# One transformer layer on one core: the norms applied by ScalarE, and a longer running sum on VectorE in one attention chunk

## The reference

```python
paths = sigmoid(x @ Wp + bp)                       # 8 heads x 5 levels
agree = pq * pk + (1 - pq) * (1 - pk)
sim   = cumprod(agree, -1).sum(-1) / 5             # causal mask, then
ctx   = softmax(sim) @ (x @ Wv)
x = layernorm(x + ctx @ Wo)
h = silu(x @ wg.T) * (x @ wu.T)                    # 768 wide
x = layernorm(x + h @ wd.T)
# layernorm(x) = (x - mean) / sqrt(var + 1e-5), over the 256 columns
```

## Time and profile before

| what | value |
|---|---|
| median of 3 runs | 849.27 us (848.09 to 849.35) |
| the profiled execution's own time | 848.94 us |
| its span | 847.1 us |
| PE busy | 802.3 us (95%) |
| DVE busy | 613.9 us (72%) |
| ACT busy | 456.4 us (54%) |
| POOL busy | 293.4 us (35%) |

### The profile page before, as it was taken

How to read it: one execution, slowest core, us unless ns; L and a number is a source line. 1 busy time by engine, 2 the same in 40 slices (tenths; PEclk the granted TensorE clock), 3 DMA queues, 4 the chain that set the end, 5 groups by cost and what they waited for, 6 DMA issues and landing times.

```text
span 847.1 us, 14414 instructions
## 1 busy us (share of the span) xinstructions
PE 802.3 (95%) x5538; PEld 397.6 (47%) x5538; DVE 613.9 (72%) x1101; ACT 456.4 (54%) x721; POOL 293.4 (35%) x266
## 2 busy tenths in 40 slices
PE   6998999999999999999999999999999998999886
PEld 5553364444634455453644536444454444444253
DVE  2767966778667876679666795677766787667966
ACT  1656736556465654657455573655646464465422
POOL 0201522436225262244413462142622425234424
PEclk9999999999999999999999999999999999999998
DMA  7932462042610636006630247105260063400001
GB/s 226 208 105 75 100 160 91 1 103 77 171 50 1 150 83 166 1 6 146 147 102 1 60 91 186 64 1 117 84 150 1 1 150 91 109 1 2 26 0 52
DMA packets 47510, 71.02 MB, mean 84 GB/s; under 512 B 3920, under 2 KB 26704, under 8 KB 47440
## 3 DMA queue, kind: packets, MB, share of 16 engines
q1 hardware_dynamic: 47440, 70.07, 31.7%
HBM read 53.28 MB, written 16.78 MB: 83 GB/s over the span
## 4 chain that ended last, share of the span: by engine, by line
PE 57%; DVE 25%; issue 9%; ACT 5%; POOL 1%; DMA 1%; SPq 0%; DVEq 0%; POOLq 0%; ACTq 0%
PE slot L879 10%; PE misc L960 9%; PE ctx_ps L902 9%; PE misc L853 7%; PE misc L948 7%; PE misc L925 6%; DVE acc L600 5%; PE den_ps L908 5%; DVE work L700 5%; ACT probs L504 4%; DVE x L683 3%; DVE acc L597 3%; DVE x1T_lo L690 2%; PE misc L862 2%; DVE ctx_raw L610 1%
## 5 line engine op out<-in xcount | busy, mean ns | idle before, releaser
L504 ACT ACTIVATE probs<-slot 128x1024 f32<-128x1024 f32 (+3 forms) x384 | 290.2, 808 | 290.4 <-PE slot L879 261.9
L433 POOL TENSOR_SCALAR_AFFINE_SELECT probs<-probs 128x512 f32<-128x512 f32 x128 | 145.9, 1140 | 207.7 <-ACT probs L504 207.5
L447 POOL TENSOR_TENSOR work<-work 128x512 f16<-128x512 f32 x96 | 116.1, 1209 | 177.4 <-ACT work L522 177.4
L902 PE MATMUL ctx_ps<-probs,vz_sb 128*32 128x512 f32 (+3 forms) x1536 | 164.5, 501 | 4.8 <-DVE ctx_raw L610 2.6
L879 PE MATMUL slot<-query_stack,key_stack 128*128 128x512 f16 (+3 forms) x768 | 160.6, 330 | 1.6 <-ACT probs L504 1.0
L948 PE MATMUL misc<-x1T_hi,w_parts 128*128 128x512 f16 x358 | 136.1, 380 | 8.5 <-DVE x1T_lo L690 6.0
L948 PE MATMUL misc<-x1T_lo,w_parts 128*128 128x512 f16 x358 | 135.8, 379 | 0.0
L879 PEld LDWEIGHTS slot<-query_stack,key_stack 128*128 128x128 f16 x768 | 56.6, 98 | 161.6 <-issue 126.2
L600 DVE TENSOR_TENSOR acc<-acc,probs 128x1536 f32<-128x1536 f32 (+3 forms) x64 | 106.5, 1664 | 1.3 <-POOL probs L433 1.1
L700 DVE SCALAR_TENSOR_TENSOR work<-work,misc 128x512 f32<-128x512 f32 x90 | 61.4, 682 | 59.7 <-ACT work L516 59.7
L960 PE MATMUL misc<-w_parts,work 128*128 128x256 bf16 x720 | 84.8, 274 | 2.4 <-POOL work L447 2.0
(11 more groups left out here) (81 smaller groups left out, 738.4 us busy)
## 6 DMA issues: line engine op xcount, KB each, us to landing
key_stack<-phi_dram SPq DMA_DIRECT2D x56, 256.0 KB, 5.8
query_stack<-phi_dram SPq DMA_DIRECT2D x56, 256.0 KB, 6.6
x_sb<-in_x_dram SPq DMA_DIRECT2D x8, 1024.0 KB, 5.3
out_dram<-x SPq DMA_DIRECT2D x15, 512.0 KB, 4.5
xT_sb<-in_xT_dram SPq DMA_DIRECT2D x7, 1024.0 KB, 4.9
phi_dram<-phi_hi SPq DMA_DIRECT2D x14, 256.0 KB, 2.0
phi_dram<-phi_lo SPq DMA_DIRECT2D x14, 256.0 KB, 2.3
key_stack<-phi_dram SPq DMA_DIRECT2D x16, 128.0 KB, 3.1
```

Of the source, the lines that this page charges most:

```text
L433: pool.affine_select(out=tile, in_=tile, compare_op=ALU.is_ge, fill=0.0, base=0, pattern=[[0, 4], [1, P]], channel_multiplier=-1).then_inc ...
L447: pool.tensor_tensor(hid_lo[:, n % M1, :], hid[:, n % HSLOTS, :], hid_hi[:, n % M1, :], ALU.subtract).then_inc(hid_lo_ready, 1)
L504: act.activation(probs[:, s % P_SLOTS, 2 * p:2 * p + 2, off:CH], slot[p][:, :, off:CH], ACT.Exp).then_inc(slot_drained[p], 1)
L902: mm = pe.matmul(ctx_ps[32 * k:32 * k + 32, off:CH], vz_sb[:, b % 2, j, 32 * h:32 * h + 32], probs[:, s % P_SLOTS, k, off:CH], start=first ...
```

## The change

`apply` moves from DVE to ACT: four ACT instructions on 128x256 rows compute `rstd * x + shift`, with the two factors read from per-partition tiles. DVE makes the shift, `-mean * rstd`, in one small instruction at the place in its queue where `apply` stood. The two-row `apply_half` of the very end stays on DVE. Apart from that, `ADD_FROM` for pass 2 goes from 3 to 1.

```diff
-    ADD_FROM = {2: 3, 3: 1}
+    ADD_FROM = {2: 1, 3: 1}
...
+            def apply(ln, b, c):                       # ScalarE
+                act.wait_ge(shift_ready, NORM[ln, b, c] + 1)
+                for t in range(TC):
+                    row = x1[:, TC * c + t, :]
+                    act.activation(row, row, ACT.Identity, bias=mean_scaled[:, t:t + 1],
+                                   scale=rstd[:, t:t + 1]).then_inc(ln_done, 1)
...
-            def apply(ln, b, c):                       # VectorE
+            def shift(ln, b, c):
                 dve.wait_ge(rstd_ready, NORM[ln, b, c] + 1)
-                for t in range(TC):
-                    row = x1[:, TC * c + t, :]
-                    dve.tensor_scalar(row, row, mv[:, t, 0:1], rstd[:, t:t + 1],
-                                      ALU.subtract, ALU.mult).then_inc(ln_done, 1)
+                dve.scalar_tensor_tensor(out=mean_scaled[:, :], in0=mv[:, :, 0], scalar=-1.0, in1=rstd[:, :],
+                                         op0=ALU.mult, op1=ALU.mult).then_inc(shift_ready, 1)
```

More of the change, by code:

```diff
@@ L253, in seq_postln_kernel @@
         rstd = sb("rstd", [P, TC], F32)
+        mean_scaled = sb("mean_scaled", [P, TC], F32)
         w_max = sb("w_max", [P, 4], F32)
@@ L308, in seq_postln_kernel @@
         rstd_ready = sem("rstd_ready")
+        shift_ready = sem("shift_ready")
         ln_done = sem("ln_done")
@@ L538, in _ @@
                     hidden_hi(*n)
+                elif what == "apply":
+                    apply(*n)
         @block.vector
@@ L800, in _ @@
                 elif what == "apply":
-                    apply(*n)
+                    shift(*n)
                 elif what == "stats_half":
```

## The result

The changed kernel takes 866.78 us (median of four runs, 865.79 to 870.19) against 849.28 for the kernel before: 2.2% slower, a ratio of 1.0217 with a 95% interval of 1.0199 to 1.0235. The forecast was 857.4, with 849 to 865 as its range. The direction held and most of the places did. The size did not: +17.5 us instead of +8.1, above the range.

What follows compares the result with a forecast made beforehand. PE bounds most of a batch, with DVE's queue nearly equally long in places. Step 12's 2.8 us plus step 18's 5.9, less 0.6 in batch 0, make +8.1 us: 857.4 us, range 849 to 865.

Steps and rivals of the forecast that it cites:

- What bounds the kernel: PE sets the pace over most of a batch, DVE in places; there longer DVE or ACT chains are paid at once.
- The row: One norm row on ACT, 128x256 with both factors read from tiles: 0.46 us, 1.84 us for four.
- with two tiles at 80 ns each: Term in a norm row's price on ACT: each of two factor tiles adds 80 ns, 0.160 us together.
- Step 12: Norm rows ahead of step 13's exponentials delay L700 and PE's transposes: 0.40 us in batches 1 to 7, 2.8 us.
- Step 18: Norm rows hold step 19's exponentials, tanh and L700: 0.98 us in batches 1 to 6, 5.9 us.
- 0, give or take 0.5: Cost at step 18 of the last batch, where half the gate work leaves ACT more room.
- At steps 2 and 4 nothing hangs closely on the rows: Exponentials there are needed a step later: cost 0, up to 0.1 us a batch at step 4.
- PE's clock falls: Rival: idle PE around steps 13 to 14 drops to the lower clock every batch; 10.5 us more, 868 us; 13%.
- The sum: Whole kernel: 2.8 + 5.9 - 0.6 = +8.1 us, which makes 857.4 us.
- the first batch: Batch 0, step 12: DVE fills its wait for POOL with the addition, features come earlier: -0.6 us.
- a row at 1.3 us: Even-outcome rival, four rows on ACT near their lower end: 847.5 us at 1.08, 850.5 at 1.3; 14%.
- one at 2.3: Upper end of the forecast's own mechanism, four rows between 1.4 and 2.3 us: 851.6 to 863.3 us; 65%.

## Why the forecast was right on the place and wrong on the size

- *What bounds the kernel.* Right. PE and DVE are nearly equally long at these places, a longer chain through ACT was paid at once, and PE's saving became idle time. That the same saving brings 1.05 us a batch when the rows are out of the way shows it from the other side.
- *The row.* Priced 0.46 us, 1.84 for four; measured 0.50 and 1.98 start to start, 0.59 each by itself. The term "with two tiles at 80 ns each" was too small. The Trainium skill's price ("ScalarE: Activation LUTs", section "What ACT_TABLE_LOAD costs"), from which the forecast gave an estimate of 1.97 for four, agrees with the measured 1.98. At 14 places this is 0.14 each, 2 us.
- *Step 12*, 0.40 forecast: 0.55, of which 0.14 is the row. Right in mechanism. One thing that the forecast did not see was covered by luck: the added addition slowed POOL's rstd to 3.02 us (1.01 before). It ended at 370.75, and DVE needed it at 371.18, behind its gate pair, so 0.43 us of slack were left.
- *Step 18*, 0.98 forecast: 1.31. 0.14 is the row; 0.2 is the next addition, 2.41 us to the next start where before it took 2.20 (394.42 to 396.62). It starts at 403.36 while POOL's f16 rest of the tile before is still running (402.54 to 403.70); before, that had ended at 394.14. The last batch's step 18, put at "0, give or take 0.5", cost 1.2: its scores wait 0.73 and twice 0.3 for exponentials.
- *"At steps 2 and 4 nothing hangs closely on the rows. I take 0"*: this is the step that failed most. The next batch's features hang on one ACT instruction, the squash (L473, now L475). In before it stood at 430.61 right behind the last copy, and now it stands behind the rows. ACT's timeline at step 4, of before, then of after:

```profile
430.61 0.33 ACT L473 ACTIVATE u_sb<-z_sb 128x160 f32<-128x160 f32 x1
```

```profile
439.75 2.06 ACT L519 ACTIVATE x<-x,mean_scaled,rstd 128x256 f32<-128x256 f32 x4
441.71 0.32 ACT L475 ACTIVATE u_sb<-z_sb 128x160 f32<-128x160 f32 x1
```

  That costs 0.18 us in a middle batch. In the last batch there is no next one whose inputs PE could project in the meantime. The rows are paid whole there and the granted clock falls to 0.50 behind them: 2.6 us. ACT's timeline, and PE's:

```profile
743.96 2.07 ACT L519 ACTIVATE x<-x,mean_scaled,rstd 128x256 f32<-128x256 f32 x4
745.94 2.56 ACT L506 ACTIVATE probs<-slot 128x768 f32<-128x768 f32 x4
```

```profile
746.78 0.39 PE L888 MATMUL slot<-query_stack,key_stack 128*128 128x256 f16 x2 [1.67 <-ACT probs L506]
747.48 0.39 PE L888 MATMUL slot<-query_stack,key_stack 128*128 128x256 f16 x2 [0.30 <-ACT probs L506]
```

  The forecast had looked at the middle batches alone. With step 4's norm back on VectorE both costs are gone from the trace.
- *The rival "PE's clock falls".* It came in part: not in every batch but in four of the seven, and it did not cost the 1.5 us a batch that the forecast had put on it, but 0.4 to 0.7. (That DVE paces part of that stretch as well would explain it; this was not tried.) The stretches of after (length, then busy time of PE, PEld, DVE, ACT, POOL, and PE's granted clock, as in the earlier trace rows):

```profile
374.00:376.00 2.00, 0.79 (x4) 0.23 (x4) 0.63 (x1) 2.00 (x5) 0.69 (x2) 0.98 0.00 0
376.00:377.00 1.00, 0.79 (x4) 0.76 (x5) 0.96 (x3) 0.83 (x2) 1.00 (x1) 0.50 0.00 0
377.00:379.00 2.00, 2.00 (x14) 0.95 (x12) 2.00 (x2) 1.41 (x3) 2.00 (x2) 0.50 0.00 0
```

  PE is busy 0.79 of 2 us, then the clock drops to 0.50, the lower level, and the transposes that follow take 1.94 us. As a consequence of the waits it should have had a term of its own, not an all-or-nothing rival. This count is that of the traced run, whose granted clock averaged 0.982; the other runs of after had 0.986 to 0.988, so theirs was probably smaller.
- *The sum.* With the measured terms in place of the forecast's, 3.9 + 9.1 + 1.1 + 2.6 + 2.1 - 1.0 + 1.2 = 19 us for the traced run; between the medians there are 17.5. Of what the forecast's +8.1 lacked, 3.7 are step 4, 3.2 step 18, 2.1 the clock, 1.1 step 12, and 1.2 the end of the program, which had no term; the first batch took 0.4 off. Two of the prediction's rival sums are also off by 0.2: a row at 1.3 us gives 850.3, and one at 2.3 gives 863.5.

## What to carry to other kernels

Before moving work to an engine that looks idle, find what stands behind the new place in that engine's queue and who waits for it. Here one norm's rows a little later in the queue, a second norm at another step and a third back on VectorE turned 2.2% slower into 1.2% faster. Walk every place where the moved instruction is issued, the last batch above all, where the filler that hides it in the middle is missing. Work taken from the bounding engine is worth nothing until the next chain is shorter as well. And read a move by the parts of the program, not by its total: two differences of 3 to 4 us cancelled in one run here.

## What was not expected of the hardware

- DVE and POOL hold each other off: the same addition took 2.20 or 3.16 us start to start, POOL's f16 rest 1.16 or 3.26 us, the 128x4 rstd 1.01 or 3.02 us, by which of the two had started first, by 0.03 to 0.14 us.
- ScalarE's 128x256 instruction takes 0.40 us with a constant factor and 0.59 with a scale and a shift from tiles.
